# Ten blocks of expert up-products moved into the second half of a head-parallel attention (Trainium2, one core)

## The reference, cut to what matters

```
x = x + LN(attention(LN(x)))        # 16 heads, 1024 x 1024 scores per head and batch
x = x + LN(experts(LN(x)))

def per_group(xf, lw, lb):          # 4 groups of 1024 tokens (a quarter of each sequence)
    combine, dispatch = top2_dispatch(xf, Wg, C)     # 24 experts, C = 86
    h = moe_apply(xf, combine, dispatch, W1, b1)     # 128 -> 512, summed over a token's two experts
    h = relu(layer_norm(h, lw, lb))
    return moe_apply(h, combine, dispatch, W2, b2)   # 512 -> 128
```

## Time and profile before

| | us |
|---|---|
| median of 3 runs | 1120.83 |
| lowest, highest | 1110.16, 1125.5 |
| span of the profiled execution | 1135.4 |
| of it the second attention (first to last exponential) | 239.5 to 728.3 |
| of it the expert layers | 728.3 to 1135.4 |

### The profile page before, as it was taken

How to read it: one execution, slowest core, us unless ns; L and a number is a source line. 1 busy time by engine, 2 the same in 40 slices (tenths; PEclk the granted TensorE clock), 3 DMA queues, 4 the chain that set the end, 5 groups by cost and what they waited for, 6 DMA issues and landing times. The chain is left out here.

```text
span 1135.4 us, 19356 instructions
## 1 busy us (share of the span) xinstructions
PE 908.8 (80%) x6642; PEld 428.2 (38%) x6642; DVE 580.1 (51%) x1969; ACT 774.8 (68%) x1130; POOL 353.7 (31%) x335
## 2 busy tenths in 40 slices
PE   3959878859999999998999999887876488477830
PEld 3745664312222222222222233224563265357730
DVE  7499998931144444444342624255214036476667
ACT  1236555789999999999999999746444254455510
POOL 6322445831000000000000013147746735365733
PEclk9669988969999999999999999998889688898975
DMA  5000001544541211212121213668747436375741
GB/s 166 1 1 1 1 1 50 130 111 153 154 118 43 61 42 40 56 36 54 44 62 44 58 36 83 184 188 198 143 127 229 88 114 178 95 192 156 144 118 51
DMA packets 91325, 106.56 MB, mean 94 GB/s; under 512 B 12957, under 2 KB 63902, under 8 KB 91114
## 3 DMA queue, kind: packets, MB, share of 16 engines
q1 hardware_dynamic: 77512, 76.83, 22.9%
q0 software_dynamic: 12224, 27.80, 12.0%
q10 hardware_dynamic: 1506, 0.89, 0.3%
HBM read 68.90 MB, written 36.57 MB: 93 GB/s over the span
## 5 line engine op out<-in xcount | busy, mean ns | idle before, releaser
L1676 ACT ACTIVATE s_e<-s_ps 128x1024 f32<-128x1024 f32 x512 | 476.7, 1065 | 12.3 <-PE s_ps L1846 11.5
L1859 PE MATMUL s_acc<-s_e,s_v 128*32 128x512 f32 x2048 | 274.0, 607 | 0.7 <-ACT s_e L1676 0.7
L1293 POOL DMA_INDIRECT x_in<-x_tokens,rows_of x72 | 72.2, 1003 | 458.7 <-DVE rows_of L1449 416.3
L1846 PE MATMUL s_ps<-qk 51*128 51x512 bf16 x1024 | 180.2, 387 | 23.1 <-ACT s_e L1676 10.4
L1846 PEld LDWEIGHTS s_ps<-qk 51*128 51x128 bf16 x1024 | 41.2, 93 | 272.8 <-ACT s_e L1676 252.2
L2291 ACT ACTIVATE qk<-e_pn,ln_hid 128x384 f32<-128x384 f32 x96 | 63.4, 667 | 89.7 <-remote 38.9
L2196 PE MATMUL e_py<-w,qk 128*96 128x128 f32 x768 | 112.3, 298 | 0.5 <-issue 0.5
L2166 PE MATMUL e_ph<-w,qk 128*32 128x512 f32 x576 | 84.9, 654 | 31.9 <-ACT e_hs L2259 23.9
L2196 PEld LDWEIGHTS e_py<-w,qk 128*96 128x96 f32 x768 | 101.6, 184 | 0.8 <-issue 0.8
L1293 POOL DMA_INDIRECT e_ya<-y_rows,take x64 | 63.0, 985 | 40.5 <-issue 19.4
L2259 ACT ACTIVATE e_hs<-e_ph,gate_of 128x512 f32<-128x512 f32 x54 | 36.3, 687 | 56.8 <-PE e_ph L2169 31.3
(11 more groups left out here) (459 smaller groups left out, 1422.7 us busy)
## 6 DMA issues: line engine op xcount, KB each, us to landing
h_rows<-e_hs SPq DMA_DIRECT2D x54, 256.0 KB
w<-in_w SPq DMA_DIRECT2D x10, 768.0 KB, 6.1
qk<-parts_k SPq DMA_DIRECT2D x64, 96.0 KB
qk<-parts_k SPq DMA_DIRECT2D x64, 64.0 KB
h_rows<-x_res SPq DMA_DIRECT2D x16, 256.0 KB
parts_q<-b_parts SPq DMA_DIRECT2D x16, 192.0 KB, 2.8
parts_k<-b_parts SPq DMA_DIRECT2D x16, 192.0 KB, 2.8
qk<-parts_q SPq DMA_DIRECT2D x64, 48.0 KB
```

Source lines behind the costliest of these rows:

```text
L1293: nc.gpsimd.indirect_dma_start(dst, None, rows, bass.IndirectOffsetOnAxis(ap=idx, axis=0), compute_op=op).then_inc(R["landed"][k % FLIGHT] ...
L1676: nc.scalar.activation(E[g % 4][:, 2 * pair:2 * pair + 2, :], pS[BUFFER["score", 2 * g + pair]][:].rearrange("p (a s) -> p a s", a=2), ACT ...
L1846: last = nc.tensor.matmul(pS[BUFFER["score", 2 * g + pair]][:, a * CH:(a + 1) * CH], K[c % 2][rows, pair, j * P:(j + 1) * P], Q[c % 2][row ...
L1859: last = nc.tensor.matmul(acc[hu % 2][32 * h:32 * h + 32, :], V4[c % 2][:, j, h, :], E[g % 4][:, h, :], start=j == 0, stop=j == TB - 1)
```

## The change

Blocks 0 to 9 (`UB = 10`) have their up layers inside halves 5 to 7 of the attention. To have a bank, both attention outputs use one accumulator from unit 18 on (`SINGLE`); the other, `spare`, serves the routing of groups 0 and 1, which moves to steps 160 to 184, and then, from step 186, a transpose of x or a product tile in steps 0, 2, 4, 5 and 7 of each eight (`UP_STEPS`, 40 in all). DVE copies the x transpose into `XT` (in `v_all`) and scales each product into one of four staging tiles in `x_res` (`up_read`); GpSimd stores them to `h_rows`. After the attention SP loads the own rows back into the ring (`own_load`), then GpSimd adds the partners. The expert stage starts with block 0, has up layers 10 to 23 at new places, and normalises up to three blocks ahead across groups. Blocks 6 and 7 join the accumulated ones. W1 is centred in halves 1 to 3, nine experts a half; the late part of W2 is loaded from half 6 on; the unrolled part on PE begins at half 4.

```diff
+UB = 10
+UNROLLED = 4
+SINGLE = UNROLLED * HU + 2
+ROUTE_STEPS = {"places": (160, 162), "rows": ((170, 172), (181, 183)), "tiles": (173, 184)}
+UP_STEPS = [s for s in range(186, G * HB) if s % TB in (0, 2, 4, 5, 7)][:UB * (TPB + 1)]
+NST = 4
...
+        acc_of = lambda k, hu: acc[0] if single(k, hu) else acc[hu % 2]
+        spare = acc[1]
+        XT = R["V"][:, 0:NQ].rearrange("p n t e -> p (n t e)")[:, 0:TPB * P]
+        staged = [R["X"][:, b * TB:b * TB + TH, :].rearrange("p t d -> p (t d)") for b in range(NST)]
...
+                if n == 6 * NQ + 1:
+                    sp.wait_ge(split_done, 6)
+                    sp.wait_ge(R["rows_done"], 2)
+                    w2(slice(EARLY, NE))
...
             for n in range(NXS):
                 gather_x(nc, R, n)
-                landed(pool, R, place("x", 0, TPB * n + TPB - 1))
+            for n in range(UB):
+                for t in range(n * TPB, (n + 1) * TPB):
+                    pool.wait_ge(u_read, t + n + 2)
+                    nc.gpsimd.dma_start(DR["h"][t // NT][t % NT, :, :], staged[t % NST]).then_inc(R["st_out"][t % NST], 16)
+                if n + NXS < 2 * NB:
...
+                    gather_x(nc, R, n + NXS)
...
+            def up_read(step):
...
+                v.wait_ge(u_mm, i + 1)
+                if j < 0:
+                    nc.vector.tensor_copy(XT, spare[:, 0:TPB * P]).then_inc(u_read, 1)
+                    return
...
+                if t >= NST:
+                    v.wait_ge(R["st_out"][t % NST], 16 * (t // NST))
+                nc.vector.tensor_scalar(staged[t % NST], spare[:], R["G128"][:, t // NT, t % NT:t % NT + 1], None,
+                                        ALU.mult).then_inc(u_read, 1)
...
+            def early_up(step):
...
+                    pe.wait_ge(u_read, i)
...
+                up_products(nc, R, spare, XT, n, j).then_inc(u_mm, 1)
...
-                    if g >= 2 or not first:
+                    if unrolled and g % TB == 3:
+                        av(k, first, g - 3)
+                    if not unrolled and (g >= 2 or not first) or unrolled and g % TB != 2:
                         av(k, first, g - 2)
...
-        ACCUMULATED = (0, 1, 2, 3, 4, 5, 11, 17, 21, 22, 23)
+        ACCUMULATED = (0, 1, 2, 3, 4, 5, 6, 7, 11, 17, 21, 22, 23)
...
+            return {1: (10,), 2: (11,), 5: (12,), 6: (13, 14), 7: (15, 16), 8: (17,)}.get(m, (m + 9,) if 9 <= m <= 14 else ())
...
+            def own_load(n):
+                if n >= NR:
+                    sp.wait_ge(hn_mm, FC * (n - NR + 1))
+                for m in range(n * TPB, (n + 1) * TPB):
+                    sp.dma_start(row(m), DR["h"][n // NB][m % NT, :, :]).then_inc(own_in[n], 16)
```

More of the change, by code:

```diff
@@ new lines, in route @@
+                for h in range(2):
+                    if step == ROUTE_STEPS["rows"][h][0]:
+                        pe.wait_ge(R["hot_done"], 2 * (h + 1))
+                        if h == 0:
+                            pe.wait_ge(R["pos_read"], 2)
+                        else:
+                            pe.wait_ge(R["rows_done"], h)
+                        map_products(nc, R, W, spare, h, range(GT))
+                    if step == ROUTE_STEPS["rows"][h][1]:
+                        map_products(nc, R, W, spare, h, range(GT, 2 * GT))
+                    if step == ROUTE_STEPS["tiles"][h]:
+                        last_products(nc, pe, R, W, spare, h)
@@ L2395, in output, with added_behind @@
                 nc.vector.tensor_tensor(x, x, y, ALU.add).then_inc(o_done, 1)
+            def added_behind(m):
+                for b in (2 * NB, 3 * NB):
+                    if m + 4 == b:
+                        return
+                    if m + 3 == b:
+                        added(b)
+                if m + 4 < NU:
+                    added(m + 4)
             p = HB - 1
```

545 lines of the change are left out of this document (294 added, 251 removed), and 4 rows, old and new, of the table STAGES.

## The result

The median went from 1119.82 us (4 runs) to 1150.86 us (4 runs, 1148.6 to 1153.78): ratio 1.0291, 95% interval 1.0238 to 1.0344. The change makes the kernel slower; the prediction said 1068. The profiled execution took 1150.36 us, its span is 1148.6.

The account below looks back on a forecast made before the run. The prediction took ACT to bound the attention (PE after the change) and read the expert layers off GpSimd's nearly serial queue. Attention +29 and experts -82 gave -53, so 1120.83 - 53 = 1068 us, range 1028 to 1115.

Parts of the forecast that it names:

- The inserted work, +29: Attention: 40 inserted steps make units PE-bound, 18.2 us against 15.3, +23, plus 6 for the bank; bounds +18 to +57.
- the 6 us for the bank: Attention: insertions share one PSUM bank that DVE must read between products; 0.8 us a unit, +6.
- Rivals A and C: Attention: A, each insertion waits for DVE, +55, 1094 us, chance 0.14; C, PE's stops starve ACT, +80, 1156 us, 0.13.
- The 30 stores and 24 more gathers ... I cost these at nothing: Attention: the added stores and gathers go on POOL's queue, which stands idle there, and cost nothing.
- First result 39 us into the stage: Expert layers: block 0's result about 39 us in, against 70 before; 31 of the 82 us gained.
- I read the gain off GpSimd, the only queue whose work is nearly in series: Expert layers: GpSimd's work, start, end and waits sum to 325 us against 407, -82; bounds -115 to -20.
- The sum 251: Expert layers: GpSimd's 133 plain and 39 accumulating gathers, with 12 us more, take 251 us; before 277.
- The waits inside: Expert layers: GpSimd's waits, some 110 us before, fall to 48: border waits go, two thirds of the other 71 stay.
- The three borders (39 us) go: Expert layers: GpSimd's waits for stores at group borders vanish, 39 us, as products are done well before.
- The loads, -82 or -70: Expert layers: own loads from SP, 7.9 MB more, would slow the first partners; -82 would then be -70.
- the 12 us of the prediction's sentence: Expert layers: were each of the first six blocks to take 2 us longer, -82 would be -70.
- Rival B: Expert layers: stalls belong to dense traffic and come back; experts gain only 45, attention +29, 1105 us; chance 0.17.

Follow-up runs that it names:

- e5: Kernel after, with a GpSimd memset of a 480-column scratch tile before each gather (gathers 1.64 us apart): 1132.7 us, ratio 1.0108 to before.
- e15: Kernel before, without the line that makes GpSimd wait for each trio of its first twelve x gathers to land: 1130.2 us, ratio 1.0076.
- e10: Kernel after, with a GpSimd memset of 160 columns before each gather (gathers 1.36 us apart): 1123.5 us, ratio 1.0055 to before.
- e8: Kernel before, with a GpSimd memset of 480 columns before each gather: 1110.3 us, ratio 0.9898.
- e6: Kernel after, with the wait for each early trio of x gathers restored and blocks 10 and 11 made right behind the attention: 1144.6 us, ratio 1.0232.
- e9: Kernel of e5, with blocks 10 and 11 made at once behind the attention: 1135.4 us, ratio 1.0153 to before.
- e17: Kernel of e10, with blocks 10 and 11 made at once behind the attention: 1130.8 us, ratio 1.0101 to before.
- e13: Kernel of e10, with each load of own rows joined by a DRAM-to-DRAM copy of the same rows: 1142.7 us, ratio 1.0176 to before.
- e16: Kernel of e10, with all matmuls of each early product tile left out but one bf16 one of the bias: 1113.2 us, ratio 0.9933 to before.

## Why the prediction was wrong, point by point

1. **The inserted work, +29: right in sum.** Without the stop the attention ends at 759.2 (e5), 31 us later than 728.3; the prediction said 757. The split was off: a product tile takes PE 1.21 us (656.81 to 658.02), not 1.08, and the 6 us for the bank don't show, since PE is busy 163.66 of 163.90 us. With 1.21 us a tile and 0.48 us for the transposes the prediction's own sum for PE gives 27.5 us; the other 3 to 4 of the 31 have no named source, so that the total came within 2 us is in part luck. Rivals A and C had the wrong mechanism; that the time fell beside C's 1156 is chance.
2. **"The 30 stores and 24 more gathers ... I cost these at nothing": the first step that failed.** GpSimd's queue had room for them, as the prediction said. But the diff took away GpSimd's wait for each trio. What the gathers cost is not on their own queue: 12 to 14 us in the attention (771.0 and 773.0 against 759.2 in e5; +10 by the one line in e15).
3. **First result 39 us into the stage: nearly right.** 43.4 (44.3 in e10) against 70, 22 to 27 of the 31.
4. **"I read the gain off GpSimd, the only queue whose work is nearly in series": the step that failed most, with 51 of the 82.** The sum 251 held: 198.27 busy and 0.30 between two of 172 gathers is 250. The waits inside did not. They were set at 48; those of at least 1.5 us, without the start, add up to 99. So the 51 us forecast for the blocks behind the first result came out at 2.4 between the first and last result, and by the estimate above perhaps at a loss. In before GpSimd's queue was no bound either: e8 puts 0.4 us on each of its 196 gathers, 78 us in all, and the kernel gets 9 us faster (1110.3 against 1119.4). A queue with 110 us of waiting is one link of a ring.
5. **"The three borders (39 us) go": wrong.** They measured 42.9 (31.3 before; the 39 was a misreading of the earlier trace rows, with group 0's wait in it and two waits taken for one border). The buffers had been overlooked: the ring of 27 tiles is nine blocks, so up layers 10 and 11 follow blocks 1 and 2 and still come before the partners of block 6 can be asked for. Taking the first away by another order of loads won nothing that can be told (e6, e9, e17), in part because that order has waits of its own.
6. **The loads, -82 or -70.** By the Trainium skill ("Trainium Kernel Development and Optimization", section "Key Constraints") DMAs of all issuing engines share 16 DMA engines; the trace agrees, their share is 0.93 in the first 50 us (770 to 820), where loads of SP and gathers of GpSimd run together. Whether the loads cost the 12 us of the prediction's sentence stays open: in e13 twice the loads cost 21 us, but with SP's queue lengthened as well, and the first result came only 3 us later.
7. **Rival B came nearest, with half of the mechanism.** It said that the unnamed stalls would come back, which they did (78.2 us of ACT's waits against 66.9), and laid them to the dense traffic; the runs show that it is how closely GpSimd's gathers follow each other, and not how much is moved. It let the experts keep a gain of 45 us; by the spans it was 29.5, and it had not seen that the same thing could reach the attention. The rows gave reason for a larger chance than 0.17: 38.9 us of unnamed waits at one line were the largest wait of ACT in that stage, and the prediction priced the two thirds of its "waits inside" without knowing what they were.

What stays open: what sets the 11.8 us per block that both kernels show at 1.36 us between gathers (271.4 and 272.9 us for 23 blocks). It is not the first border wait alone, and that it is GpSimd's queue is not shown. What the own loads cost, and what the 14 us of e16 are, is open too. Nor was it tried by which path close gathers hold up the other engines; "signals" in the theory's words is a guess at it. That they do, and at what distance it fades, is shown.

## What to carry to other kernels

Before a queue with idle time is called free, ask what its instructions do to the other engines; here gathers of GpSimd in unbroken succession stopped three of them. Waits with no named releaser on several engines at once are a cause to be found before anything is predicted, and the first thing to lay beside them is what the one engine that still runs is doing. And a gain is not to be read off one queue of a ring of engines that all wait: test first, with a cheap lengthening of that queue, whether it bounds. And before stages of two profiled executions are compared, lay their spans beside the medians: here that turns a gain of 29.5 us behind the attention into one of some 12.

## What the runs showed of the hardware

- Indirect DMAs of GpSimd 1.25 us apart hold up PE, ACT and DVE from about the fifth on (574.5 to 584 beside twelve; one stop of 3.5 us beside six; none beside three with pauses of 2.4 us). At 1.36 us apart about half of it is left, at 1.64 nothing in the attention. Their rows had 512 bytes there; in the expert layers, where some have 2 KB, ACT's unnamed waits were 78, 39 and 0 us at the same three distances.
- A memset on GpSimd before each gather made two kernels faster, by 20.7 and 9 us. It isn't free beside DVE: DVE's busy time in the expert layers rose from 193 to 215 us with 480 columns and to 196 with 160. The Trainium skill's page "SBUF — State Buffer" (section "SBUF: two separate sides") has the two engines share a port; these rows agree. Not all of DVE's work is touched: its scaling of a 128x512 tile (TENSOR_SCALAR) went from 506 to 670 ns, the addition of two (TENSOR_TENSOR) stayed at 688.
- Four fp32 products of 32 rows each in one tile take PE 1.06 us, one of them 1.05 us.
- While PE stood, its granted clock went from 1.00 (until 574) to 0.50 (from 577 on), and it was still 0.50 from 586 to 589, with PE busy 2.74 of 3 us.
